# A convolution stage on one core: variances queued a step ahead of their powers, and logits written to another PSUM bank

## The chip, the core and the metric

The kernel runs on one core of a Trainium2 chip. The core has five engines that work in parallel and meet through semaphores: TensorE (PE in the profile; PEld is its loading of weights), VectorE (DVE), ScalarE (ACT), GpSimd (POOL) and SyncE (SP), which issues most of the DMAs. Each engine takes its instructions in the order in which they were queued: one that waits holds up all behind it. The metric is the device time of one execution in microseconds; lower is better.

## What is computed

Four layers, each a normalized input that goes through a block and is added to the residual:

```python
x = x + _L0_xattn_ref(_layernorm(x), L0_xattn_k, fside_S2_0, ctx_2048, ctx_2048, 8)
x = x + _L0_ffn_ref(_layernorm(x), L0_ffn_gate_w, ...)     # 8 experts, the best 2 of each token, and a shared one
x = x + _L1_xattn_ref(_layernorm(x), ctx_2048, itok_BxS_0_1023, ...)
x = x + _L1_ffn_ref(_layernorm(x), L1_ffn_proj1, ...)
```

The change lies in the first layer and the router of the second. The first is a long convolution, written in the reference with Fourier transforms:

```python
kv = vr[:, :, :, None, :] * x2r[:, :, None, :, :]
y = irfft(rfft(kv, n=fft_size) * k_f[None, :, None, None, :], n=fft_size)[..., :L]
y = y + kv * skip
out = jnp.einsum('bhijl,bhil->bhjl', y, x1r)
```

The layer norm is `(x - m) / sqrt(v + eps)`. The router's logits are `logits = xf @ gate_w`, 512 by 8.

## The kernel before

Data are 4096 rows of 512. The convolution works on 32 heads, a tile of 128 rows each, and is done as matmuls with a Toeplitz matrix of the filter. A head has two halves (u = 0, 1), and a half four blocks (lb = 0 to 3) of 128 positions. For a block, conv takes 3 matmuls for each of the first two input blocks (high and low parts, line 387) and one full-precision matmul, recorded as two, for each further one (line 382). VectorE then multiplies the result from PSUM (z, line 394) and sums it (line 400).

The inputs of the matmuls are made ahead. GpSimd makes the products kf (line 355), five blocks ahead of their use. ScalarE rounds two of four into kh (line 362), and the remainder kl (line 370) is subtracted by VectorE for the first block and by GpSimd for the second.

In the same queues run, for head h+1, the filter (lines 300 to 312), the norm and the transposes (turn, line 332, into bank PV), for head h+2 the loads and the variance (stats), and for head h-1 the end of the layer: finish transposes the result into bank PR (line 405) and adds it to the residual (line 407). Its output is normalized again for the router: stats0 makes the variance, shift0 the shift nm0 (line 472), norm0 the rows xb (line 476), turn0 transposes them into PV (line 483). A head later logit multiplies them by the gate (line 490, into PV) and ScalarE copies the 8 logits out (line 492); best takes the largest (lines 501, 502), and choose, in heads 9, 17 and 25, turns eight tiles of them into experts and gates.

A variance is three VectorE instructions (lines 120 to 122: statistics over 512 elements, their aggregate, plus epsilon) and a GpSimd power of -0.5 (line 123). layernorm_stats queues all four at once, in stats at u = 1, lb = 2, and in stats0 at u = 1, lb = 0.

The order is that of the Python loop over h, u and lb: each step calls the functions, and each call appends to its engine's queue. Dependencies are tokens (a semaphore and its value). `T` and `U` keep the last token under a name; `U["PV",]` and `U["PR",]` hold the last reader of the two banks, for which the next writer waits. After the last head a second loop (line 791 on) starts the shared expert, with the remains of the convolution queued as events between its steps; there PR also takes the transposes of line 631 (turn1), and line 638 empties it.

Of the kernel before, what the change touches and what calls it, by code (L numbers as in the profile page):

```python
# [11 lines left out]
ALU = mybir.AluOpType  # L12
ACT = mybir.ActivationFunctionType
# [5 lines left out]
EPS = 1e-5  # L19
# [92 lines left out]
def make_identity(p, ident):  # L112
    a = p.do("gpsimd", lambda e: e.memset(ident, 0.0))
    return p.do("gpsimd", lambda e: e.affine_select(out=ident, in_=ident, compare_op=ALU.not_equal, fill=1.0, base=0,
                                                    pattern=[[-1, 128]], channel_multiplier=1), a)


def layernorm_stats(p, x, st, ag, rs, mhalf, tok, free, c):

    a = p.do("vector", lambda e: e.bn_stats(st, x), tok, free)  # L120
    a = p.do("vector", lambda e: e.bn_aggr(ag, st), a)
    a = p.do("vector", lambda e: e.tensor_scalar(rs, ag[:, 1:2], EPS, None, ALU.add), a)
    return p.do("gpsimd", lambda e: e.tensor_tensor(rs, rs, mhalf, ALU.pow), a, c)
# [3 lines left out]
def front_phase(nc, ctx, d, before, xa, idx, gat, ident, mhalf, n_heads=NHC):  # L127


    p = Phase(nc, ctx, "c", before)  # L130
    keep = Mem(nc, ctx, "f")
    LAG, NG, NB, RING = 5, NT // 2, 4, 5
    U = {}

    def gu(*k):
        return U.get(k)
# [27 lines left out]
    xt = m.sb("xt", [128, 4, 512])  # L164
# [85 lines left out]
    T = {}  # L250
# [5 lines left out]
    def clear(n):  # L256

        for c in left[:n]:
            U["clr",] = p.dma("sync", dz, lambda e, c=c: e.dma_start(xsz[:, c:c + 512], zero[:, :]), c_z)
        del left[:n]  # L260

    def g(*k):
        return T.get(k)
# [27 lines left out]

    def stats(h):
        s = h % 2
        T["rs", h] = layernorm_stats(p, xt[:, h % 4, :], st[:, s, :], ag[:, s, :], rs[:, s, :], mhalf, g("x", h), g("xn", h - 2), c_mh)

    def filt(h):

        s = h % 2
        if h < 2:
            T["pt", h] = p.do("tensor", lambda e: e.matmul(PT[:, :], anti, tf[:, s, :], start=True, stop=True), g("tf", h), c_an, g("tl", h - 1))  # L300
        else:
            T["pt", h] = p.do("tensor", lambda e: e.matmul(PT[:, :], antir, tr[:, s, 0, :], start=True, stop=True), g("tf", h), c_anr, g("tl", h - 1))
        T["th", h] = p.do("scalar", lambda e: e.activation(th[:, s, :], PT[:, :], ACT.Copy), g("pt", h), g("mm", h - 2))
# [10 lines left out]
    def shift(h):  # L314
        s = h % 2
        T["nm", h] = p.do("vector", lambda e: e.tensor_scalar(nm[:, s, :], ag[:, s, 0:1], rs[:, s, :], -1.0, ALU.mult, ALU.mult), g("rs", h), g("xn", h - 2))
# [85 lines left out]
    def finish(h):  # L402
        s = h % 2
        for lb in range(4):
            T["pr", h] = p.do("tensor", lambda e, lb=lb: e.transpose(PR[:, 128 * lb:128 * lb + 128], R[:, s, lb, :], ident),
                              g("R", h), gu("PR"), inc=lb == 3)
        T["out2", h] = U["PR",] = p.do("vector", lambda e: e.tensor_tensor(xt[:, h % 4, :], sk[:, s, :], PR[:, :], ALU.add), g("pr", h), g("sk", h))
        T["out", h] = p.dma("sync", do[h % 4], lambda e: e.dma_start(d["x1"][:, 8 * h:8 * h + 8, :], xt[:, h % 4, :]), g("out2", h))
# [56 lines left out]

    def stats0(i):
        s = i % 2
        U["rs", i] = layernorm_stats(p, xt[:, i % 4, :], st0[:, s, :], ag0[:, s, :], rs0[:, s, :], mhalf, T["out2", i], gu("xb", i - 2), c_mh)

    def shift0(i):  # L470
        s = i % 2
# [15 lines left out]
    def logit(i):  # L487

        for k in range(4):
            U["pl", i] = p.do("tensor", lambda e, k=k: e.matmul(PV[:, 0:8], xT[:, k, :], gw[:, k, :], start=k == 0, stop=k == 3),  # L490
                              U["xT", i], U["c0",], gu("PV"), inc=k == 3)
        U["lg", i] = U["PV",] = p.do("scalar", lambda e: e.activation(lg[:, i // 8 % 2, i % 8, :], PV[:, 0:8], ACT.Copy), U["pl", i], gu("ix", i - 16))

    B8 = [128, 8, 8]

# [180 lines left out]
    load(0)  # L676
    load(1)
    stats(0)
    filt(0)
    filt_lo(0)  # L680
    shift(0)
# [3 lines left out]
    skips(0)  # L685
    residual(0)
    stats(1)
    shift(1)
    split_filters()
    setup()  # L690
# [5 lines left out]
    for h in range(n_heads):  # L696
        more = h + 1 < n_heads
        for u in range(2):
            for lb in range(4):
                if u == 0 and lb == 2 and h + 2 < n_heads:  # L700
                    load(h + 2)
                    clear(3)
                if u == 1 and lb == 2 and h + 2 < n_heads:
                    stats(h + 2)
                if u == 1 and lb == 0 and more:
                    filt(h + 1)
                if u == 1 and lb == 2 and more:
                    filt_lo(h + 1)
                if u == 0 and lb == 0 and more:
                    norm(h + 1)  # L710
                if u == 0 and lb == 0 and more:
                    weigh(h + 1)
                if u == 1 and lb == 3 and h + 2 < n_heads:
                    shift(h + 2)
                if u == 0 and lb == 3 and more:
                    turn(h + 1)
                n = (2 * h + u) * 4 + lb + 4
                if n + 1 < len(units):
                    product(*units[n + 1])
                if n < len(units):  # L720
                    parts(*units[n], low=False)
                conv(h, u, lb, units[n] if n < len(units) and lb == 0 else None)
                if u == 0 and lb == 3 and h:
                    finish(h - 1)
                if u == 1 and lb == 1 and more:
                    skips(h + 1)
                if u == 1 and lb == 2 and more:
                    residual(h + 1)
                if u == 0 and lb == 1:
                    shared_weights()  # L730
                    if h > 1:
                        logit(h - 2)
                if u == 0 and lb == 3 and h > 1:
                    best(h - 2)
                if u == 1 and lb == 0 and h > 8 and h % 8 == 1:
                    choose(h // 8 - 1)
                if h and u == 1:
                    (stats0, shift0, norm0, turn0)[lb](h - 1)
                if not more and u == 0:
                    fill(row(lb))  # L740
                if not more and u == 1:
                    if lb < 2:
                        loadr(lb)
                    if lb in (1, 2):
                        turn1(lb - 1)
# [14 lines left out]
    def more(n):  # L760
# [6 lines left out]
        if todo:  # L767
            src, to, c = todo.pop(0)
            pend.append((fetch(src), to, c, ("w1",) if to is w1f else ("w2",)))

    events = {0: [lambda: finish(last), lambda: logit(last - 1), lambda: stats0(last), lambda: shift0(last), lambda: norm0(last)], 1: [lambda: best(last - 1)],
              3: [lambda: turn0(last)], 4: [lambda: logit(last)], 5: [lambda: best(last), lambda: choose(3)], 7: [ranks], 8: [offsets],
              9: [places, by_head], 10: [experts], 11: [biases]}
    steps = NG * NB
# [973 lines left out]
```

How the kernel before makes its waits and increments, by code:

```python
    def emit(self, e, eng):  # L72
        seen = {}
        def wait(sem, v):
            if seen.get(id(sem), 0) < v:
                eng.wait_ge(sem, v)
                seen[id(sem)] = v
        for sem, v in self.before:
            wait(sem, v)
        for fn, waits, inc in self.q[e]:
            for w in waits:
                if w is not None:
                    wait(*w)
            ins = fn(eng) if fn else None
            if inc:
                ins.then_inc(*inc)
# [1638 lines left out]
                def run(eng, e=e):  # L1727
                    for p in phases:
                        p.emit(e, eng)
                    if e == "sync":
                        for sem, v in before:
                            eng.wait_ge(sem, v)
```

## Time and profile before

| | |
|---|---|
| median of 3 runs | 3270.91 us (3270.78 to 3271.13) |
| profiled execution, its own time | 3268.49 us |
| its span in the profile | 3266.7 us |
| mean granted TensorE clock over the span | 0.991 |
| PE busy | 3162.6 us (97%) |
| VectorE busy | 2159.1 us (66%) |
| ScalarE busy | 1261.4 us (39%) |
| GpSimd busy | 1126.1 us (34%) |

The convolution stage takes about the first 640 us, a fifth of the span. In its stretch from 300 to 400 us PE is busy 97.09 us, VectorE 87.11, GpSimd 77.22 and ScalarE 33.53, at a granted clock of 1.00. Percentages of the whole span say little of it: GpSimd's 34% is 77% here. A busy PE is not PE at its peak, because matmuls are pipelined and their ends are modelled; the distance between the starts of two matmuls is what one costs. A head is one period of this stage, so one period, read on all four engines, stands for some twenty. The queries read are the waits of an engine (whom it waited for, in all and how often), the timeline of an engine (instructions in order of time, with the idle time ahead and who ended it), and the account of a single line.

### The profile page before, as it was taken

How to read it: one execution, taken by the hardware profiler on the slowest of the kernel's cores; microseconds unless marked ns; L12 is line 12 of the kernel's file. 1: busy time of each engine (PE TensorE's matmuls, PEld its weight loads, DVE VectorE, ACT ScalarE, POOL GpSimd, SP SyncE). 2: the span in 40 equal slices, each digit the busy share in tenths (PEclk: the TensorE clock that was granted, in tenths of full speed). 3: DMA queues.
4: the chain of work that ended last, by engine and by line, in shares of the span. 5: the costliest groups of instructions: out<-in, count | busy, mean ns of one | idle time of the engine just before them, and what ended most of it. 6: DMA issues, size and time to landing. Idle time of an engine off the chain costs nothing.

```text
span 3266.7 us, 51561 instructions
## 1 busy us (share of the span) xinstructions
PE 3162.6 (97%) x18517; PEld 2687.2 (82%) x18517; DVE 2159.1 (66%) x5741; ACT 1261.4 (39%) x3041; POOL 1126.1 (34%) x1179
## 2 busy tenths in 40 slices
PE   7999999999999789999999999999998999999999
PEld 4666666689899579999999999999997888888887
DVE  6888888755555568877788888877776533333332
ACT  2333333333444345555555555555554311111111
POOL 6877777535344322222222222222201011000110
PEclk9999999999999899999999999999999999999999
DMA  4544443269677721111111111111101300000000
GB/s 127 151 142 140 132 133 103 81 198 328 214 234 225 242 72 53 46 46 46 46 46 46 45 38 42 46 46 46 34 14 55 98 26 26 26 26 26 26 14 14
DMA packets 129418, 285.92 MB, mean 88 GB/s; under 512 B 18840, under 2 KB 19488, under 8 KB 129168
## 3 DMA queue, kind: packets, MB, share of 16 engines
q1 hardware_dynamic: 100080, 186.49, 18.3%
q0 software_dynamic: 29088, 96.13, 8.9%
q8 instruction: 153, 2.51, 0.3%
q14 instruction: 97, 0.79, 0.1%
HBM read 177.98 MB, written 104.58 MB: 86 GB/s over the span
## 4 chain that ended last, share of the span: by engine, by line
PE 79%; DVE 9%; POOL 7%; DMA 2%; ACT 1%; issue 1%; SPq 0%; POOLq 0%; DVEq 0%
PE g_PH L1021 11%; PE g_O L1044 11%; PE t_U L1486 10%; PE t_S L1438 9%; PE t_PO L1473 5%; PE t_M L1422 5%; PE t_T L1460 3%; POOL c_kf L355 3%; PE f_Y L664 2%; PE f_Y L893 2%; PE t_M L1377 2%; PE f_Y L387 2%; PE f_Y L382 2%; DVE c_R L400 2%; DVE c_z L394 2%; PE t_M L1359 2%
## 5 line engine op out<-in xcount | busy, mean ns | idle before, releaser
L1448 ACT ACTIVATE t_pr<-t_sm,t_nb 128x256 f32<-128x256 f32 x512 | 256.6, 502 | 368.2 <-DVE t_nb L1444 368.2
L1392 POOL TENSOR_TENSOR t_r<-t_r 128x256 f32<-128x256 f32 x128 | 96.1, 751 | 778.9 <-DVE t_rw L1454 451.4
L1034 DVE CAST g_hh<-g_hf 128x512 fp32r<-128x512 f32 x128 | 61.8, 482 | 435.7 <-PE g_O L1044 427.0
L355 POOL TENSOR_TENSOR c_kf<-c_vt,c_ct 128x512 f32<-128x512 f32 x256 | 297.0, 1181 | 0.0
L1033 ACT ACTIVATE g_hf<-g_PH,g_b1s 128x512 f32<-128x512 f32 x128 | 88.2, 689 | 519.1 <-PE g_PH L1021 518.3
L1455 DVE TENSOR_SCALAR t_pr<-t_pr,t_rw 128x256 f32<-128x256 f32 x512 | 222.0, 434 | 18.1
L387 PE MATMUL f_Y<-c_kh,c_th 128*128 128x512 f32 x448 | 200.1, 447 | 10.5 <-ACT c_kh L362 10.5
L1021 PE MATMUL g_PH<-g_xh,g_w1h 128*128 128x512 f32 x512 | 205.8, 402 | 1.5 <-DVE g_xl L1009 1.5
L1021 PE MATMUL g_PH<-g_xh,g_w1l 128*128 128x512 f32 x512 | 203.5, 397 | 0.0
L1021 PE MATMUL g_PH<-g_xl,g_w1h 128*128 128x512 f32 x512 | 203.1, 397 | 0.0
L1044 PE MATMUL g_O<-g_w2h,g_hh 128*128 128x512 f32 x512 | 202.4, 395 | 0.0
L1044 PE MATMUL g_O<-g_w2h,g_hl 128*128 128x512 f32 x512 | 202.2, 395 | 0.0
L1486 PE MATMUL t_U<-t_voh,t_otl 128*128 128x512 f32 x512 | 201.7, 394 | 0.0
L1486 PE MATMUL t_U<-t_voh,t_oth 128*128 128x512 f32 x512 | 201.7, 394 | 0.0
L1044 PE MATMUL g_O<-g_w2l,g_hh 128*128 128x512 f32 x512 | 201.5, 394 | 0.0
L1486 PE MATMUL t_U<-t_vol,t_oth 128*128 128x512 f32 x512 | 200.9, 392 | 0.0
L1444 DVE CUSTOM_DVE_ANT_0 t_sm<-t_S,t_mk 128x256 f32<-128x256 f32 x512 | 194.6, 417 | 8.6 <-PE t_S L1438 8.6
L394 DVE TENSOR_TENSOR c_z<-f_Y,c_ct 128x512 f32<-128x512 f32 x256 | 174.0, 680 | 35.2 <-PE f_Y L382 35.0
L382 PE MATMUL f_Y<-c_kf,c_t 128*128 128x512 f32 x384 | 185.4, 591 | 0.0
L1465 DVE TENSOR_TENSOR t_ptl<-t_T,t_pth 128x512 fp32r<-128x512 f32 x256 | 175.5, 685 | 15.0 <-ACT t_pth L1464 14.8
L400 DVE TENSOR_REDUCE c_R<-c_z 128x64 f32<-128x512 f32 x256 | 174.9, 683 | 6.6
L387 PE MATMUL f_Y<-c_kl,c_th 128*128 128x512 f32 x448 | 178.1, 398 | 0.0
(345 smaller groups left out, 9706.6 us busy)
## 6 DMA issues: line engine op xcount, KB each, us to landing
xs<-c_zero SPq DMA_DIRECT2D x71, 256.0 KB, 5.2
f_xg<-xs SPq DMA_DIRECT2D x71, 256.0 KB, 3.4
ys<-f_yt POOLq DMA_DIRECT2D x71, 256.0 KB, 3.6
c_tr<-kpad SPq DMA_DIRECT2D x60, 256.0 KB, 4.7
f_xg<-xn SPq DMA_DIRECT2D x40, 256.0 KB, 4.7
c_xt<-x SPq DMA_DIRECT2D x32, 256.0 KB, 3.5
c_cr<-ctx SPq DMA_DIRECT2D x32, 256.0 KB, 4.0
c_ct<-ctxh SPq DMA_DIRECT2D x32, 256.0 KB, 4.1
```

What stands on the lines that cost most here:

```text
L355: T["kv", h] = T["kv1", n] = p.do("gpsimd", lambda e: e.tensor_tensor(o, iv, ic, ALU.mult), g("vt", h), g("ct", h), g("kl", n - 8), g("kh" ...
L382: last = p.do("tensor", lambda e, c=c, mb=mb: e.matmul(Y[y % 4][:, :], t0[:, s, c], kf[:, v, mb, :], start=False, stop=mb == lb), g("t0", ...
L387: last = p.do("tensor", lambda e, a=a, b_=b_, c=c, mb=mb, i=i: e.matmul(Y[y % 4][:, :], a[:, s, c], b_[:, v, mb, :], start=(mb == 0 and i ...
L394: T["z", h] = T["z1", y] = p.do("vector", lambda e: e.tensor_tensor(zz.rearrange("p (b j i) -> p b j i", i=8, j=8), iv, ic, ALU.mult), las ...
L400: T["red", y] = T["R", h] = p.do("vector", lambda e: e.tensor_reduce(rr, zr, AXX, ALU.add), g("z1", y), g("pr", h - 2))
L1021: T["ph", n] = p.do("tensor", lambda e, kk=kk, a=a, b_=b_, i=i: e.matmul(ph[:, :], a[:, k, kk, :], b_[:, s, kk, :], start=i == 0, stop=i = ...
L1044: tk = p.do("tensor", lambda e, a=a, b_=b_, t=t, fin=fin, c=c, beg=beg: e.matmul(O[t][:, :], a[:, n % 2, c], b_[:, k, :], start=beg, stop= ...
L1438: a = p.do("tensor", lambda e, t=t, j=j, q=q, k=k: e.matmul(PS1[:, 256 * t:256 * t + 256], q, k[:, s, :], start=j == 0, stop=j == 4), g("q ...
L1444: T["am", N] = am = p.do("vector", lambda e, t=t, k4=k4: e.tensor_tensor_reduce(out=sm[:, k4, :], in0=PS1[:, 256 * t:256 * t + 256], in1=m ...
L1448: T["ex", x] = p.do("scalar", lambda e, t=t, k4=k4: e.activation(pr[:, N % 2, t, :], sm[:, k4, :], ACT.Exp, bias=nb[:, k4, 0:1], scale=-1. ...
L1455: T["nm", x] = p.do("vector", lambda e, t=t, k4=k4: e.tensor_scalar(pr[:, N % 2, t, :], pr[:, N % 2, t, :], rw[:, k4, 1:2], None, ALU.mult ...
L1486: a = p.do("tensor", lambda e, t=t, tt=tt, j=j, o=o, w=w: e.matmul(PU[t][:, :], o[:, N % 3, tt], w[:, h, :], start=h == 0 and j == 0, stop ...
```

## The change

layernorm_variance is new: the three VectorE instructions of a variance without its power. stats and stats0 now queue only these, and new functions power and power0 queue the power on GpSimd. In the loop stats(h+2) moves from u = 1, lb = 2 to u = 1, lb = 1, and power(h+2) takes its old place. stats0(h-1) moves from u = 1, lb = 0 to directly behind finish(h-1) at u = 0, lb = 3, ahead of best, and power0(h-1) takes its old place. Shifts, norms and transposes stay where they were. The matmuls of logit and the copy behind them go to PR in place of PV. Before the loop and in the events the power follows its variance directly, as before. layernorm_stats stays for the later layers.

```diff
+def layernorm_variance(p, x, st, ag, rs, tok, free):
+
+    a = p.do("vector", lambda e: e.bn_stats(st, x), tok, free)
+    a = p.do("vector", lambda e: e.bn_aggr(ag, st), a)
+    return p.do("vector", lambda e: e.tensor_scalar(rs, ag[:, 1:2], EPS, None, ALU.add), a)
...
     def stats(h):
         s = h % 2
-        T["rs", h] = layernorm_stats(p, xt[:, h % 4, :], st[:, s, :], ag[:, s, :], rs[:, s, :], mhalf, g("x", h), g("xn", h - 2), c_mh)
+        T["va", h] = layernorm_variance(p, xt[:, h % 4, :], st[:, s, :], ag[:, s, :], rs[:, s, :], g("x", h), g("xn", h - 2))
+
+    def power(h):
+        s = h % 2
+        T["rs", h] = p.do("gpsimd", lambda e: e.tensor_tensor(rs[:, s, :], rs[:, s, :], mhalf, ALU.pow), T["va", h], c_mh)
...
     def stats0(i):
         s = i % 2
-        U["rs", i] = layernorm_stats(p, xt[:, i % 4, :], st0[:, s, :], ag0[:, s, :], rs0[:, s, :], mhalf, T["out2", i], gu("xb", i - 2), c_mh)
+        U["va", i] = layernorm_variance(p, xt[:, i % 4, :], st0[:, s, :], ag0[:, s, :], rs0[:, s, :], T["out2", i], gu("xb", i - 2))
+
+    def power0(i):
+        s = i % 2
+        U["rs", i] = p.do("gpsimd", lambda e: e.tensor_tensor(rs0[:, s, :], rs0[:, s, :], mhalf, ALU.pow), U["va", i], c_mh)
...
         for k in range(4):
-            U["pl", i] = p.do("tensor", lambda e, k=k: e.matmul(PV[:, 0:8], xT[:, k, :], gw[:, k, :], start=k == 0, stop=k == 3),
-                              U["xT", i], U["c0",], gu("PV"), inc=k == 3)
-        U["lg", i] = U["PV",] = p.do("scalar", lambda e: e.activation(lg[:, i // 8 % 2, i % 8, :], PV[:, 0:8], ACT.Copy), U["pl", i], gu("ix", i - 16))
+            U["pl", i] = p.do("tensor", lambda e, k=k: e.matmul(PR[:, 0:8], xT[:, k, :], gw[:, k, :], start=k == 0, stop=k == 3),
+                              U["xT", i], U["c0",], gu("PR"), inc=k == 3)
+        U["lg", i] = U["PR",] = p.do("scalar", lambda e: e.activation(lg[:, i // 8 % 2, i % 8, :], PR[:, 0:8], ACT.Copy), U["pl", i], gu("ix", i - 16))
...
+                if u == 1 and lb == 1 and h + 2 < n_heads:
+                    stats(h + 2)
                 if u == 1 and lb == 2 and h + 2 < n_heads:
-                    stats(h + 2)
+                    power(h + 2)
...
                 if u == 0 and lb == 3 and h:
                     finish(h - 1)
+                    stats0(h - 1)
...
                 if h and u == 1:
-                    (stats0, shift0, norm0, turn0)[lb](h - 1)
+                    (power0, shift0, norm0, turn0)[lb](h - 1)
```

## Rows read from the trace of the kernel before

**Rows 1.** PE's waits, first 1300 us: who waited for whom: total, times, longest.

```profile
PE f_PV L332 <- ACT c_lg L492: 14.2, 29, 1.2
PE f_PV L483 <- ACT c_xb L476: 1.0, 3, 0.3
```

**Rows 2.** Timeline of PE: start, us, instruction, [idle before and who ended it].

```profile
50.38 1.02 PE L382 MATMUL f_Y<-c_kf,c_t 128*128 128x512 f32 x2
51.23 0.60 PE L332 MATMUL f_PV<-ident,c_xn 128*128 128x128 f32 x4
...
397.10 1.02 PE L382 MATMUL f_Y<-c_kf,c_t 128*128 128x512 f32 x2
398.40 0.63 PE L332 MATMUL f_PV<-ident,c_xn 128*128 128x128 f32 x4 [0.28 <-ACT c_lg L492]
```

**Rows 3.** GpSimd's waits, first 1300 us.

```profile
POOL c_rs L123 <- DVE c_rs L122: 145.7, 63, 9.5
```

**Rows 4.** Timelines of PE and ScalarE behind the last head.

```profile
648.42 0.50 PE L645 MATMUL f_PSK<-f_xh,c_sw 128*128 128x256 f32 x2 [2.68 <-ACT f_hf L653]
...
658.62 0.64 PE L631 MATMUL f_PR<-ident,f_xg 128*128 128x128 f32 x4
658.80 0.18 ACT L492 ACTIVATE c_lg<-f_PV 128x8 f32<-128x8 f32 x1 [2.65 <-PE f_PV L490]
```

**Rows 5.** Timeline of VectorE, an ordinary head.

```profile
402.18 0.69 DVE L394 TENSOR_TENSOR c_z<-f_Y,c_ct 128x512 f32<-128x512 f32 x1 [0.87 <-PE f_Y L382]
403.51 0.68 DVE L407 TENSOR_TENSOR c_xt<-c_sk,f_PR 128x512 f32<-128x512 f32 x1
...
405.04 0.68 DVE L370 TENSOR_TENSOR c_kl<-c_kf,c_kh 128x512 fp32r<-128x512 f32 x1
406.24 0.68 DVE L120 BATCH_NORM_STATS2 c_st<-c_xt 128x6 f32<-128x512 f32 x1
407.17 0.15 DVE L122 TENSOR_SCALAR c_rs<-c_ag 128x1 f32<-128x1 f32 x1
407.25 0.68 DVE L394 TENSOR_TENSOR c_z<-f_Y,c_ct 128x512 f32<-128x512 f32 x1
409.16 0.21 DVE L472 TENSOR_SCALAR c_nm<-c_ag,c_rs 128x1 f32<-128x1 f32 x1
```

**Rows 6.** Timelines of PE and VectorE, the transposes of line 483 and what precedes them.

```profile
362.87 0.69 DVE L394 TENSOR_TENSOR c_z<-f_Y,c_ct 128x512 f32<-128x512 f32 x1 [0.87 <-PE f_Y L382]
371.27 0.20 DVE L472 TENSOR_SCALAR c_nm<-c_ag,c_rs 128x1 f32<-128x1 f32 x1
372.38 0.66 PE L483 MATMUL f_PV<-ident,c_xb 128*128 128x128 f32 x4 [0.32 <-ACT c_xb L476]
...
392.26 0.60 PE L483 MATMUL f_PV<-ident,c_xb 128*128 128x128 f32 x4
411.21 0.60 PE L483 MATMUL f_PV<-ident,c_xb 128*128 128x128 f32 x4
```

**Rows 7.** Timeline of VectorE behind the last head: a variance directly on its sum.

```profile
643.04 0.69 DVE L407 TENSOR_TENSOR c_xt<-c_sk,f_PR 128x512 f32<-128x512 f32 x1 [0.88 <-PE f_PR L405]
643.76 0.69 DVE L120 BATCH_NORM_STATS2 c_st<-c_xt 128x6 f32<-128x512 f32 x1
```

**Rows 8.** Timeline of GpSimd, the same ordinary head.

```profile
407.41 0.55 POOL L123 TENSOR_TENSOR c_rs<-c_rs,mhalf 128x1 f32<-128x1 f32 x1 [4.06 <-DVE c_rs L122]
407.92 1.07 POOL L355 TENSOR_TENSOR c_kf<-c_vt,c_ct 128x512 f32<-128x512 f32 x1
```

**Rows 9.** VectorE and GpSimd together; last, line 370's durations: ns min/median/max, first and last start.

```profile
14.03 0.75 DVE L325 SCALAR_TENSOR_TENSOR c_w<-c_xn,c_skip,c_cr 128x512 f32<-128x512 f32 x1 [0.88 <-ACT c_xn L320]
...
393.73 1.29 POOL L346 TENSOR_TENSOR c_sk<-c_sk,c_xt 128x512 f32<-128x512 f32 x1
394.23 1.34 DVE L325 SCALAR_TENSOR_TENSOR c_w<-c_xn,c_skip,c_cr 128x512 f32<-128x512 f32 x1
...
L370 DVE TENSOR_TENSOR c_kl<-c_kf,c_kh x64: 679/876/955, 26.4 to 624.8; 128x512 fp32r<-128x512 f32 x64
```

More of the change, by code:

```diff
@@ L678, in front_phase @@
     stats(0)
+    power(0)
     filt(0)
@@ L687, in front_phase @@
     stats(1)
+    power(1)
     shift(1)
@@ L769, in more @@
             pend.append((fetch(src), to, c, ("w1",) if to is w1f else ("w2",)))
-    events = {0: [lambda: finish(last), lambda: logit(last - 1), lambda: stats0(last), lambda: shift0(last), lambda: norm0(last)], 1: [lambda: best(last - 1)],
+    events = {0: [lambda: finish(last), lambda: logit(last - 1), lambda: stats0(last), lambda: power0(last), lambda: shift0(last), lambda: norm0(last)], 1: [lambda: best(last - 1)],
               3: [lambda: turn0(last)], 4: [lambda: logit(last)], 5: [lambda: best(last), lambda: choose(3)], 7: [ranks], 8: [offsets],
```

## The prediction

> **What bounds the kernel now.** I read the waits of TensorE (PE) first, because PE is busy nearly all of the time: what it waits for is what there is to gain. In the convolution stage (27 to 640 us) one wait recurs: the first transpose of a head's values (line 332) waits 29 times, 14.2 us in all, for ScalarE's copy of the logits (line 492), which must leave bank PV first [rows 1]. The wait is more than it lists, since the ends of matmuls are modelled. Without a stall the transposes start 0.85 us after the pair of matmuls ahead of them (50.38 to 51.23); in head 20 it is 1.30 us (397.10 to 398.40) and the row lists 0.28 of idle [rows 2]. So a stall costs PE the listed idle plus 0.17: 14.2 + 29 x 0.17 = 19.1 us. The second PE wait, the transposes of line 483 for ScalarE's xb, comes 3 times, 1.0 us in all [rows 1], by the same rule 1.0 + 3 x 0.17 = 1.5 us. All stalls that this change can touch cost 20.6 us, or 0.63% of the run.
>
> Why are the logits late? ScalarE takes its work in order, and ahead of that copy stand two copies of kf (kh, line 362) that wait for GpSimd. GpSimd waits 145.7 us in 63 waits for the variance (line 122), which is nearly all its idle time [rows 3]: its power (line 123) stands behind a VectorE sum that was queued only a moment earlier. So GpSimd is late, kh is late, the logits are late, and PE waits.
>
> **The new bank.** Logits go to PR. PR's last user is then the residual sum (line 407) of half a head earlier, long done, and the transposes of line 332 need no logits any more; the next user of PR, the transposes of line 405, comes just ahead of z, over 3 us later than line 332 (398.40 to 402.18) [rows 2, 5], when the copy has ended. This alone removes the 19.1 us. It costs something only in the tail: logits of the last head are followed at once by transposes into PR (line 631). They start at 658.62, while the copy runs from 658.80 for 0.18 [rows 4]; they must now wait until about 659.05. I take 0.45 us, between 0.2 (if part is hidden) and 0.9 (the copy's own wait doubled). The logits of head 30 now wait for the residual sum of head 31 as well, about 1.0 us; PE idles 2.68 us soon after for a reason that stays [rows 4], which hides it. Without that cover it would be 1.0 us.
>
> **The variances.** No instruction is added; what counts is order. Times below are from the start of VectorE's product z of the fourth block (402.18), which begins as PE ends that block, so it is PE's clock [rows 5]. Call it z. From z the following are fixed on PE: the transposes of line 483 are due at 411.21, z+9.03 [rows 6]. They need xb, xb needs the shift nm0 (line 472), and nm0 stands at z+6.98 (409.16) [rows 5]. Where nm0 is late, the chain is to be seen: nm0 at 371.27, transposes at 372.38, so nm0 + 1.11 [rows 6]. Nm0 may be at z+7.92 at the latest: a cover of 0.94 us.
>
> Ahead of nm0 VectorE had one variance, that of x1 (stats0). Now it has two, since stats(h+2) moves from behind nm0 to ahead of it. A variance takes 406.24 to 407.25 = 1.01 us. And stats0 now follows directly on the sum that it reads, where a step is 0.72 (643.04 to 643.76) [rows 7] in place of 0.60 (half of 405.04 to 406.24, two steps) [rows 5]. Together 1.13, so nm0 is at z+8.11, the transposes at z+9.22, and PE stalls 0.19 us in a head.
>
> **What GpSimd does with its freedom.** The sum of line 407 starts at z+1.33. Stats0 starts at z+2.05, and its last step is 0.93 later (406.24 to 407.17) at z+2.98 [rows 5]. The power follows 0.24 later (407.17 to 407.41), the next product kf 0.51 after that (407.92) and it lasts 1.07 [rows 8]: GpSimd multiplies from z+3.73 to z+4.80. Before, it was idle then. VectorE comes from z+2.98 in 0.08 to the next instruction, and then over the best logits and the next block's product to its kl (line 370): 1.53 between 403.51 and 405.04, less the sum's own step of 0.60, is 0.93. So kl starts at z+3.99 [rows 5]. kl reads two tensors of SBUF. How such an operation fares beside GpSimd is in the trace: line 325 takes 0.75 us beside an idle GpSimd (14.03), but 1.34 when it starts at 394.23, inside a GpSimd sum that runs from 393.73 to 395.02; it ends 0.55 after that sum's end [rows 9]. So it waited for the whole GpSimd operation. kl itself is 0.68 us at least and 0.88 in the median [rows 9], and the one of our place is a short one (405.04, 0.68) because GpSimd was idle [rows 5]. Now it will start 0.26 after a GpSimd product and end at 4.80 + 0.55 = z+5.35 in place of z+4.67: 0.68 us more. All that follows moves with it, nm0 to z+8.79, the transposes to z+9.90: PE stalls 0.87 us in a head. Bounds: 0.19, if kl gets through unharmed, and 1.1, if it waits for all of 1.07 of the product and its own full 0.68 counts from there.
>
> The Trainium skill ("SBUF — State Buffer", section "Who interferes with whom") says the same and speaks against this change: a VectorE instruction with two SBUF inputs contends with a GpSimd instruction that reads SBUF, and whoever issues first keeps the shared interface for its whole length. By this rule, the trace agrees (0.59 us more on line 325), the term is 0.87 a head; a notion of shared bandwidth, which the page rejects, would give a stall between 0.19 and 0.87.
>
> **The sum.** Line 483 comes in heads 1 to 31 (and once in the tail). Heads 30 and 31 have no stats(h+2), so nm0 is 1.01 earlier and there is no stall. In head 1 there are no best logits yet, kl and kf meet almost at once: 0.4 us (0 to 0.87). Heads 9, 17 and 25 also choose experts between kl and nm0: nm0 at 371.27 less z at 362.87 is 8.40, 1.42 more than 6.98 [rows 5, 6], so there the stall is 2.29, and up to 1.1 more if a small two-input operation of the choice meets GpSimd too; I take 2.85. The other 25 heads stall 0.87 each. 25 x 0.87 = 21.8, 3 x 2.85 = 8.5, 0.4, and the tail 0.5: 31.2 us of new stalls against 20.6 removed. Net +10.6 us. Everything else in the 25 heads has room: GpSimd's next product of line 355 must be there when PE ends a fourth block, and it arrives over 1 us early; kh and kl are ready microseconds ahead of PE. After 670 us nothing is changed and the rest moves as a block. The profiled execution took 3268.49 us (span 3266.7), 2.4 below the median of the runs; 3268.5 + 10.6 = 3279.1 for it, and for the median 3270.9 + 10.6 = **3281.5 us**.
>
> **Rivals.**
> 1. *No collision.* GpSimd's product or VectorE's kl yields, or kl gets its turn first. For it: the lead is only 0.26 us, of which VectorE's claim, made as its preceding operation ends, gives back perhaps 0.1. Against it: both paths start at the same instruction (rs, z+2.98), so the lead doesn't drift. Stalls: 25 x 0.19 + 3 x (0.19 + 1.42) + 0.5 = 10.1; net -10.5, 3260.4 us. Faster, 0.32%.
> 2. *Partial collision.* kl loses about 0.3 us: stall about 0.5 in 25 heads, 1.9 in three, 18.8 with the tail; net -2, 3269 us.
> 3. *No stall at line 483 at all*: xb is through in time though two variances stand ahead of it. Only the 20.6 us go: 3251 us. Against it speak the three heads in which nm0 at z+8.40 stalls PE now [rows 6].
> 4. *A worse collision*: the choice's operations and the second variance meet GpSimd as well, 1.1 a head: 25 x 1.1 + 3 x 3.6 + 0.9 = 39; net +19, 3289 us.
> The forecast is itself the slower side: VectorE's path from z to nm0 takes PE's place as the bound. It decides as soon as a head's stall exceeds (20.6 - 0.5 - 3 x 1.42) / 28 = 0.57 us, that is, nm0 later than z+8.49.
>
> **Numbers.** Forecast 0.61 (3276 to 3287); no collision 0.20 (3258 to 3264); partial 0.09; never a stall 0.04; worse 0.06. A measurement of this kernel tells about 0.2% (6.5 us) from no change. Faster 0.25, same 0.12, slower 0.63. The range leaves out the last two rivals and the fast end of the first: 3259 to 3287; the forecast's own range is 3276 to 3287.
>
> **What would show it.** Right: no wait of line 332 for line 492 any more; PE waits of line 483 for xb in some 28 heads, 0.7 listed (0.87 less 0.17); the distance of two heads 19.37 us (before: 18.95, from 392.26 to 411.21 [rows 6]; less the stall of 0.45 that is 18.50, and with the new one 19.37); GpSimd's waits for the variance down from 145.7 to about 100; kl of line 370 at z+4.0 lasting some 1.35 in place of 0.68; line 631 waiting for line 492 once. Wrong: kl at 0.68 and heads 18.7 apart mean rival 1; heads 18.5 apart mean rival 3. If line 332 still waits for ScalarE, the new bank doesn't do what it says. If the heads agree and the total doesn't, the difference arose after 670 us, which I hold to be a block.

## The result, and the profile after

| | before | after |
|---|---|---|
| median of 5 runs beside each other | 3271.13 us (3270.78 to 3277.41) | 3290.61 us (3283.76 to 3291.07) |
| profiled execution, its own time | 3268.49 us | 3290.61 us |
| its span | 3266.7 us | 3288.9 us |
| mean granted clock over the span | 0.991 | 0.988 |

The change makes the kernel slower: the ratio is 1.0052, with an interval of 1.004 to 1.0063 (13 to 21 us). The medians differ by 19.5 us where 10.6 were forecast. The forecast had the side and, in the ordinary heads, the mechanism; the size was too small by 8.9 us, and a step was missing.

Line numbers grow by 11 in the convolution (332 is now 343, 370 is 381, 394 is 405) and by 15 in the code of the values (472 is 487, 476 is 491, 483 is 498, 492 is 507, 501 is 516). The powers have lines 305 (of stats) and 483 (of stats0).

The waits of TensorE (PE) from 0 to 670 us; the columns are who waited for whom, the sum in us, how often, and the longest in us:

```profile
PE f_PV L498 <- ACT c_xb L491: 27.0, 28, 3.2
...
PE f_PR L505 <- DVE c_xt L418: 0.9, 1, 0.9
```

The wait of line 332 for the logits [rows 1] is gone. In its place stands the one that was forecast: the transposes of line 498 wait for xb, 28 times in place of 3. The 0.9 are the logits of head 30, which wait for the residual sum (1.0 was forecast, under cover). The waits of GpSimd in the same stretch:

```profile
POOL c_rs L483 <- DVE c_mx L516: 67.0, 30, 6.0
...
POOL c_rs L305 <- DVE c_rs L122: 19.6, 30, 2.2
POOL c_rs L483 <- DVE c_rs L122: 11.2, 1, 11.2
```

Together these are 97.8 us, where [rows 3] had 145.7. (Releasers are inferred; line 516 stands directly behind the variance on VectorE and is named in its place.) GpSimd did get its work earlier. This is what it met there: one stretch of head 20, with the start, the duration, and in brackets the idle time ahead and who ended it; on GpSimd, VectorE and PE.

```profile
396.65 0.55 POOL L483 TENSOR_TENSOR c_rs<-c_rs,mhalf 128x1 f32<-128x1 f32 x1 [2.10 <-DVE c_mx L516]
397.16 1.06 POOL L366 TENSOR_TENSOR c_kf<-c_vt,c_ct 128x512 f32<-128x512 f32 x1
...
397.42 1.35 DVE L381 TENSOR_TENSOR c_kl<-c_kf,c_kh 128x512 fp32r<-128x512 f32 x1
398.19 1.72 POOL L381 TENSOR_TENSOR c_kl<-c_kf,c_kh 128x512 fp32r<-128x512 f32 x1
...
402.21 0.21 DVE L487 TENSOR_SCALAR c_nm<-c_ag,c_rs 128x1 f32<-128x1 f32 x1
...
403.32 0.66 PE L498 MATMUL f_PV<-ident,c_xb 128*128 128x128 f32 x4 [0.70 <-ACT c_xb L491]
...
409.07 0.60 PE L343 MATMUL f_PV<-ident,c_xn 128*128 128x128 f32 x4
```

VectorE's kl starts 0.26 us after GpSimd's product and takes 1.35 us in place of 0.68 [rows 5]; it ends 0.55 us after that product. The shift nm0 (line 487) starts 1.11 us before the transposes, as in [rows 6], and PE lists 0.70 us of idle time. Line 343 waits for nobody here. Ordinary heads are now 19.38 to 19.40 us apart; 19.37 was forecast. Up to here every step held.

Heads 9, 17 and 25, which also choose experts, did not. They are 23.39, 26.16 and 23.44 us long (a head is counted from one group of transposes of line 416 to the next). Two things are in the trace of head 9. First, the last small operation of the choice:

```profile
215.28 1.27 POOL L381 TENSOR_TENSOR c_kl<-c_kf,c_kh 128x512 fp32r<-128x512 f32 x1 [2.29 <-ACT c_kh L373]
...
215.39 1.19 DVE L534 TENSOR_TENSOR f_gac<-c_sm,f_gac 128x8 f32<-128x8 f32 x1
...
220.53 0.66 PE L498 MATMUL f_PV<-ident,c_xb 128*128 128x128 f32 x4 [3.15 <-ACT c_xb L491]
```

This is a two-input operation on 8 values a partition; the same line takes 0.17 us in the last choice (683.27). It takes 1.19 us here and ends as GpSimd's subtraction kl (line 381) ends, so the stall is 3.15 + 0.17 = 3.32 us, where 2.85 was taken. Second, what PE's matmuls cost after that wait, from PE's timeline:

```profile
221.25 0.40 PE L398 MATMUL f_Y<-c_kh,c_tl 128*128 128x512 f32 x1
221.49 0.40 PE L398 MATMUL f_Y<-c_kl,c_th 128*128 128x512 f32 x1
221.72 0.58 PE L398 MATMUL f_Y<-c_kh,c_th 128*128 128x512 f32 x1
222.10 0.63 PE L398 MATMUL f_Y<-c_kh,c_tl 128*128 128x512 f32 x1
```

and the account of two stretches of 2 us (length, then busy time and instructions of PE, PEld, VectorE, ScalarE and GpSimd, granted clock, DMA share, GB/s):

```profile
222.00:224.00 2.00, 2.00 (x6) 1.53 (x6) 1.83 (x3) 1.67 (x3) 2.00 (x3) 0.50 0.89 240
224.00:226.00 2.00, 2.00 (x12) 1.86 (x11) 2.00 (x4) 0.18 (x1) 2.00 (x2) 0.70 0.98 208
```

The same matmul starts 0.235 us after the one ahead of it at first and 0.43 later: the granted clock is 0.50 (1.2 GHz) from about 221.8, where it was 1.00 (2.4 GHz) all through this stage before. What it costs is what a choosing head is longer than an ordinary one, less the longer wait: 23.39 - 19.39 - (3.15 - 0.70) = 1.55 us in head 9, 4.32 in head 17 and, with a wait of 3.19, 1.56 in head 25, some 7.4 us in all. This is one execution; the five of this kernel took 3283.76 to 3291.07 us, so the cost need not be the same in each.

### The profile page after: what moved, and what is told of

Its sections match the earlier page's. It is cut to its first block, busy times and chain, and to the rows that moved or that the text cites. A ratio compares the mean times of both kernels' runs of the same rounds, so it can differ in the third digit from the quotient of the medians.

```text
span 3288.9 us, 51591 instructions
## 1 busy us (share of the span) xinstructions
PE 3169.1 (96%) x18517; PEld 2690.8 (82%) x18517; DVE 2182.6 (66%) x5741; ACT 1258.6 (38%) x3041; POOL 1138.1 (35%) x1179
## 3 DMA queue, kind: packets, MB, share of 16 engines
q1 hardware_dynamic: 100080, 186.49, 18.1%
## 4 chain that ended last, share of the span: by engine, by line
PE 83%; DVE 10%; DMA 2%; POOL 2%; ACT 1%; issue 1%; SPq 0%; POOLq 0%; DVEq 0%
PE g_PH L1041 11%; PE g_O L1064 11%; PE t_U L1506 10%; PE t_S L1458 9%; PE f_Y L398 6%; PE t_PO L1493 5%; PE t_M L1442 5%; PE t_T L1480 3%; PE f_Y L393 3%; PE f_Y L913 2%; PE f_Y L679 2%; PE t_M L1397 2%; DVE c_R L411 2%; PE t_M L1379 2%; DVE c_z L405 2%; PE f_PSK L882 1%
## 5 line engine op out<-in xcount | busy, mean ns | idle before, releaser
L366 POOL TENSOR_TENSOR c_kf<-c_vt,c_ct 128x512 f32<-128x512 f32 x256 | 286.2, 1132 | 44.9 <-PE f_Y L393 33.4
L1475 DVE TENSOR_SCALAR t_pr<-t_pr,t_rw 128x256 f32<-128x256 f32 x512 | 222.8, 435 | 18.1
L1485 DVE TENSOR_TENSOR t_ptl<-t_T,t_pth 128x512 fp32r<-128x512 f32 x256 | 175.5, 686 | 15.0 <-ACT t_pth L1484 14.8
L398 PE MATMUL f_Y<-c_kh,c_tl 128*128 128x512 f32 x448 | 179.5, 401 | 0.0
```

The source lines that it names most:

```text
L366: T["kv", h] = T["kv1", n] = p.do("gpsimd", lambda e: e.tensor_tensor(o, iv, ic, ALU.mult), g("vt", h), g("ct", h), g("kl", n - 8), g("kh" ...
L398: last = p.do("tensor", lambda e, a=a, b_=b_, c=c, mb=mb, i=i: e.matmul(Y[y % 4][:, :], a[:, s, c], b_[:, v, mb, :], start=(mb == 0 and i ...
L1475: T["nm", x] = p.do("vector", lambda e, t=t, k4=k4: e.tensor_scalar(pr[:, N % 2, t, :], pr[:, N % 2, t, :], rw[:, k4, 1:2], None, ALU.mult ...
L1485: T["ptl", N] = p.do("vector", lambda e: e.tensor_tensor(ptl[:, N % 2, :, :], v, f32(pth[:, N % 2, :, :]), ALU.subtract), T["pth", N], g(" ...
```

## The experiments

All were timed in 5 rounds beside the kernel before. Each diff is against the kernel that is named; "after" is the changed kernel. The theory is: a VectorE operation with two inputs in SBUF waits until a GpSimd product that started ahead of it has ended (A), and it is this, with the second variance, that makes nm0 late.

### The bank alone

Before, with the logits in PR and the variances where they were.

```diff
-            U["pl", i] = p.do("tensor", lambda e, k=k: e.matmul(PV[:, 0:8], xT[:, k, :], gw[:, k, :], ...
+            U["pl", i] = p.do("tensor", lambda e, k=k: e.matmul(PR[:, 0:8], xT[:, k, :], gw[:, k, :], ...
-        U["lg", i] = U["PV",] = ... PV[:, 0:8] ...
+        U["lg", i] = U["PR",] = ... PR[:, 0:8] ...
```

> The kernel before with the logits in PR and nothing else. Theory A (the new bank takes away the stalls of 19.1 us; the loss of the whole change is VectorE's path to nm0, held up by a collision with GpSimd): line 332 waits for nobody, heads are 18.50 apart (before 18.95), line 483 waits only in the three choosing heads, 0.3 listed, kl of line 370 stays at 0.68 beside an idle GpSimd; 3271 - 19 + 0.5 = about 3252 us, ratio 0.994. Theory B (the loss comes from the bank: finish waits for the logits, or PR is in somebody's way): slower than before, and line 405 waits for line 492.

3248.79 us (3245.45 to 3250.34), ratio 0.9936 [0.9923, 0.995]. Ordinary heads are 18.47 us apart, the choosing ones 19.02. PE's waits of that kernel, with before's line numbers:

```profile
PE f_PV L483 <- ACT c_xb L476: 1.0, 3, 0.3
PE f_PR L490 <- DVE c_xt L407: 0.9, 1, 0.9
PE f_PR L631 <- ACT c_lg L492: 0.4, 1, 0.4
```

So the bank's half of the change is worth what the profile of before said for it: 19.1 us of stalls at line 332, less 0.45 in the tail. The last logits come 19.7 us earlier in the profiles (638.12 in place of 657.81), and the medians differ by 20.9 us (before took 3269.66 beside it; the interval is 16 to 25). The 1.0 us of line 483 stays, and the tail pays 0.4 once. This version beats both kernels. Its granted clock is 1.00 throughout the stage, though the choice stands where it stood.

### The variances alone

After, with the logits back in PV.

```diff
-        U["lg", i] = U["PR",] = ... PR[:, 0:8] ...
+        U["lg", i] = U["PV",] = ... PV[:, 0:8] ...
```

> The changed kernel with the logits back in PV: the variances alone. Theory A: GpSimd is early, so kh and the logits are early too and the transposes of values don't wait in spite of the shared bank; heads 19.39 apart and three long stalls of 3.3 us as in the whole change; 3289 to 3291 us, ratio 1.005 to 1.006. Theory B (the bank did the harm): about 3260 us, heads 18.7 apart.

3286.75 us (3284.02 to 3289.31), ratio 1.005 [1.0036, 1.0063]. Heads are 19.40 us apart, the choosing ones 24.45, 26.11 and 23.44. Line 343 does not wait for the logits here either. So the whole loss belongs to the variances, and beside them the bank is worth nothing that these times show. The logits are copied soon enough in the shared bank too. First the kernel before, then this one (matmuls of the logits, their copy, the next transposes into PV; the transposes of before, at 398.40, are in [rows 2]):

```profile
394.81 0.95 PE L490 MATMUL f_PV<-c_gw,c_xT 128*128 128x8 f32 x8
398.10 0.16 ACT L492 ACTIVATE c_lg<-f_PV 128x8 f32<-128x8 f32 x1
...
427.33 0.95 PE L505 MATMUL f_PV<-c_gw,c_xT 128*128 128x8 f32 x8
428.32 0.18 ACT L507 ACTIVATE c_lg<-f_PV 128x8 f32<-128x8 f32 x1 [0.23 <-PE f_PV L505]
...
430.48 0.60 PE L343 MATMUL f_PV<-ident,c_xn 128*128 128x128 f32 x4
```

The copy came 3.29 us behind its matmuls and comes 0.99 behind them now, because ScalarE no longer waits long for GpSimd's products; it has ended 2.0 us before the transposes. The variances alone remove the wait that the bank removes. That is why the effects of the two halves (-21 and +17 us) do not add up.

### Kl ahead of z

After, with VectorE's kl queued ahead of the product z in the second half's first block, so that it no longer meets GpSimd's product.

```diff
-                    parts(*units[n], low=False)
-                conv(h, u, lb, units[n] if n < len(units) and lb == 0 else None)
+                    parts(*units[n], low=u == 1 and lb == 0)
+                conv(h, u, lb, units[n] if n < len(units) and lb == 0 and u == 0 else None)
```

> The changed kernel, but in the second half's first block kl stands ahead of z in VectorE's queue: same instructions, kl starts 0.3 us ahead of GpSimd's product in place of 0.26 behind it. Theory A (whoever starts first keeps the port): kl lasts 0.68, GpSimd's product is the longer one (about 1.3 in place of 1.07), nm0 at z+8.24, stall 0.32, heads 18.8 apart; choosing heads stall 2.7; 3267 us without clock losses, 3275 with those of the whole change, ratio 0.999 to 1.001. Rival C (the two engines slow each other by sharing bandwidth, whatever the order): kl still 1.0 or more, heads above 19.1, 3280 us or more.

3267.72 us (3264.32 to 3268.8), ratio 0.9994 [0.9985, 1.0003]; heads 18.85 us apart, as expected.

```profile
403.62 0.55 POOL L483 TENSOR_TENSOR c_rs<-c_rs,mhalf 128x1 f32<-128x1 f32 x1 [2.10 <-DVE c_mx L516]
...
403.81 0.67 DVE L381 TENSOR_TENSOR c_kl<-c_kf,c_kh 128x512 fp32r<-128x512 f32 x1
...
404.14 1.27 POOL L366 TENSOR_TENSOR c_kf<-c_vt,c_ct 128x512 f32<-128x512 f32 x1
...
404.40 0.68 DVE L405 TENSOR_TENSOR c_z<-f_Y,c_ct 128x512 f32<-128x512 f32 x1
```

Kl comes first now and takes 0.67; it is GpSimd's product that takes 1.27 in place of 1.06. The product z, which reads one input from PSUM, runs beside GpSimd in 0.68. Stalls that remain are 0.1 listed in ordinary heads and 2.6 in the choosing ones, which are 22.73, 21.30 and 21.34 us long.

### The product behind kl

After, with the power of stats0 behind GpSimd's next pair of products, so that VectorE's queue stays as the change has it and only GpSimd's order differs.

```diff
                     parts(*units[n], low=False)
+                if h and u == 1 and lb == 1:
+                    power0(h - 1)
...
-                    (power0, shift0, norm0, turn0)[lb](h - 1)
+                    (lambda i: None, shift0, norm0, turn0)[lb](h - 1)
```

> The changed kernel with the power of stats0 queued on GpSimd behind the next product and remainder in place of ahead of them: GpSimd works through while VectorE makes the variance, and has nothing but the power to do when kl comes. VectorE's queue is exactly that of the changed kernel. Theory A (0.68 of the stall of 0.87 is the collision, 0.19 the second variance): kl 0.68, heads 18.7 apart; choosing heads stall 2.6 and lose clock; 3266 to 3270 us, ratio 0.999 to 1.000. Rival G (the stall is VectorE's longer queue, the long kl only a by-product): heads stay at 19.4.

3266.62 us (3264.25 to 3270.96), ratio 0.9983 [0.9974, 0.9992]; heads 18.71 apart. VectorE and GpSimd at the same place:

```profile
403.71 1.27 POOL L381 TENSOR_TENSOR c_kl<-c_kf,c_kh 128x512 fp32r<-128x512 f32 x1 [0.24 <-ACT c_kh L373]
404.94 0.55 POOL L483 TENSOR_TENSOR c_rs<-c_rs,mhalf 128x1 f32<-128x1 f32 x1
...
405.32 0.68 DVE L381 TENSOR_TENSOR c_kl<-c_kf,c_kh 128x512 fp32r<-128x512 f32 x1
```

VectorE has the same instructions in the same order, and kl has 0.68 again; each head loses 0.68 us of its length (19.39 to 18.71). This is the collision's price alone. The clock falls behind all three choosing heads here (waits of 2.48, 2.48 and 2.53), which are 22.70 to 22.74 us long.

### Each variance back in its place

First after with stats(h+2) back at u = 1, lb = 2:

```diff
-                if u == 1 and lb == 1 and h + 2 < n_heads:
-                    stats(h + 2)
                 if u == 1 and lb == 2 and h + 2 < n_heads:
+                    stats(h + 2)
                     power(h + 2)
```

> The changed kernel with the variance of the loads, stats(h+2), back behind nm0: only stats0 is early. Theory A: the collision of kl stays (kl 1.35), but nm0 is 1.01 earlier, at z+7.78, under the z+7.92 that is free; so no wait of line 498 in ordinary heads, heads 18.5 apart. Choosing heads stall 2.3, with the clock falling behind them at a cost of 1.5 to 4.5 each. 3257 to 3262 us, ratio 0.996 to 0.9975. Rival F (an early stats0 alone is what costs): heads above 19.

3269.23 us (3266.09 to 3272.25), ratio 0.9992 [0.9983, 1.0001]; heads 18.77 to 18.87 us apart, where 18.5 was expected. Kl collides as in the changed kernel (1.35). PE lists 0.17 us of wait for xb in five early heads and none in the ordinary ones from the tenth on; yet most of these are 18.78 us long, 0.31 more than the 18.47 of the kernel with the bank alone. The stall is there all the same; the modelled end of the matmuls ahead hides it:

```profile
436.71 0.60 PE L416 MATMUL f_PR<-ident,c_R 128*128 128x128 f32 x4
...
437.31 0.68 DVE L405 TENSOR_TENSOR c_z<-f_Y,c_ct 128x512 f32<-128x512 f32 x1
...
445.07 0.21 DVE L487 TENSOR_SCALAR c_nm<-c_ag,c_rs 128x1 f32<-128x1 f32 x1
...
446.18 0.66 PE L498 MATMUL f_PV<-ident,c_xb 128*128 128x128 f32 x4
```

The transposes of line 498 start 1.11 us behind nm0, as where they wait for xb, and laid beside the same head of the kernel with the bank alone PE loses its 0.31 us at this place and nowhere else. From VectorE's z to nm0 it is 7.76 us, as expected (7.78). But z starts 0.60 us behind PE's transposes of line 416 here, and 0.20 behind them in the changed kernel (393.23 and 393.43): VectorE is late before the count begins. It is so because GpSimd waits for the second variance, now right behind nm0 on VectorE, and VectorE then waits for kh, which ScalarE makes from GpSimd's late product:

```profile
408.81 0.55 POOL L305 TENSOR_TENSOR c_rs<-c_rs,mhalf 128x1 f32<-128x1 f32 x1 [2.57 <-DVE c_rs L122]
...
414.50 0.88 DVE L381 TENSOR_TENSOR c_kl<-c_kf,c_kh 128x512 fp32r<-128x512 f32 x1 [1.03 <-ACT c_kh L373]
```

VectorE has no other idle time in a head there: it no longer waits for PE ahead of the fourth block's product, as it does in after for 1.54. VectorE, GpSimd and ScalarE seem to form a loop of 18.8 us; this is read from the rows and was not tried on its own. The expectation's 18.5 is wrong because it took VectorE's z for PE's clock; its statement that the second variance costs nm0 1.01 us holds (8.78 from z in the changed kernel, 7.76 here).

Then after with stats0 back at the head of the second half:

```diff
                     finish(h - 1)
-                    stats0(h - 1)
...
                 if h and u == 1:
+                    if lb == 0:
+                        stats0(h - 1)
```

> The changed kernel with stats0 back in its old place, its power behind it: only stats(h+2) is early. Theory A: GpSimd is held by stats0 again until after kl, so kl lasts 0.68 and there is no collision; nm0 at z+7.99, a stall of 0.07 and heads 18.55 apart; choosing heads stall 1.5 without a loss of clock; 3255 to 3259 us, ratio 0.9955 to 0.997. The collision theory fails if kl is still long here, or if kl is 0.68 and heads are 19 apart.

3255.86 us (3251.57 to 3259.19), ratio 0.9953 [0.9939, 0.9967]; heads 18.59, choosing ones 20.02. GpSimd waits for the variance again, its product starts late, and kl is alone:

```profile
396.59 0.55 POOL L483 TENSOR_TENSOR c_rs<-c_rs,mhalf 128x1 f32<-128x1 f32 x1 [3.96 <-DVE c_rs L122]
...
412.82 0.68 DVE L381 TENSOR_TENSOR c_kl<-c_kf,c_kh 128x512 fp32r<-128x512 f32 x1
```

Taking the move of stats0 back is worth 35 us (3290.61 to 3255.86), though this move only makes a variance earlier. That is more than 28 stalls of 0.87: it takes in the three choosing heads and their clock. But neither move does the harm by itself. With the logits in PR, and each beside its own runs of before, the kernel with neither move is 20.9 us faster, with the variance of the loads early 16.5, with stats0 early 3.2, and with both it is 19.5 slower. So early stats0 costs 17.7 us alone and 36.0 beside the other move: the second variance uses up the time that would have covered the collision. The choosing heads stall PE here for 1.33 us as listed, and the clock stays at 1.00 from 100 to 600 us.

### Where the clock went

The account of the choosing heads left 7.4 us that were seen but not explained. After, with the choice three blocks later:

```diff
-                if u == 1 and lb == 0 and h > 8 and h % 8 == 1:
+                if u == 1 and lb == 3 and h > 8 and h % 8 == 1:
                     choose(h // 8 - 1)
```

> The changed kernel with the choice of experts queued in the last block of the second half, behind nm0, in place of the first. Theory D (of the 19.5 us lost, some 15 belong to the three choosing heads: a stall 2.45 us longer than elsewhere, and TensorE's clock at 0.50 for 3 to 9 us after it): the choosing heads are 19.39 apart like the others, the granted clock is 1.00 there, 3275 to 3279 us, ratio 1.0015 to 1.0025. Rival E (the clock falls at those places for another reason than the long stall): the clock still falls between 200 and 560 us, and 3284 us or more.

3281.07 us (3278.55 to 3290.11), ratio 1.0038 [1.0025, 1.0052], a miss. The wait for xb is 0.7 everywhere, but ScalarE's exponential of the choice now stands ahead of the copy xT, and two small VectorE operations are held by GpSimd on the way to it:

```profile
221.06 0.95 DVE L524 CAST c_sm<-c_ix 128x16 f32<-128x16 uint32 x1
222.04 0.99 DVE L525 TENSOR_TENSOR c_sm<-c_mx 128x8 f32<-128x8 f32 x1
...
223.81 1.60 PE L505 MATMUL f_PR<-c_gw,c_xT 128*128 128x8 f32 x8 [1.76 <-ACT c_xT L500]
225.26 0.77 PE L398 MATMUL f_Y<-c_kh,c_th 128*128 128x512 f32 x1
225.84 0.63 PE L398 MATMUL f_Y<-c_kh,c_tl 128*128 128x512 f32 x1
```

A new long wait, and the clock fell after it (0.63 for a matmul in place of 0.40). The profile is of an execution of 3289.47 us, 8.4 above the median, so what the clock costs there need not be typical. This tells nothing against the theory that a long wait lowers the clock, and doesn't show it either. Next, the choice behind norm0 in the third block:

```diff
-                if u == 1 and lb == 0 and h > 8 and h % 8 == 1:
-                    choose(h // 8 - 1)
...
                     (power0, shift0, norm0, turn0)[lb](h - 1)
+                if u == 1 and lb == 2 and h > 8 and h % 8 == 1:
+                    choose(h // 8 - 1)
```

> The changed kernel with the choice of experts in the third block of the second half, behind nm0 and behind ScalarE's xb. Unlike the try in the last block, ScalarE's exponential then hardly holds up the copy that the logits wait for. Theory D: no PE wait above 1 us in the choosing heads, the granted clock stays at 1.00 from 100 to 600 us, heads 9, 17 and 25 are at most 20 us apart from the next; 3274 to 3279 us, ratio 1.001 to 1.003. If the clock still falls without a long wait, the clock losses have another cause.

3285.42 us (3281.35 to 3288.28), ratio 1.0045 [1.0031, 1.0058], a miss for the same reason. Three of the choice's operations, each 0.17 to 0.22 in the changed kernel, waited for GpSimd products one after another:

```profile
218.65 0.99 DVE L525 TENSOR_TENSOR c_sm<-c_mx 128x8 f32<-128x8 f32 x1
219.56 1.15 DVE L528 TENSOR_TENSOR c_oh<-c_iota,c_sm 128x64 f32<-128x64 f32 x1
220.64 1.10 DVE L529 TENSOR_TENSOR c_oh<-c_iota,c_sm 128x64 f32<-128x64 f32 x1
```

VectorE carried the 4 us into the next head, whose transposes waited 2.91, and there the clock fell. Last, the choice cut in three parts (copy, difference and exponential; the comparisons and their sum; the gates), one in each of three following heads, at a place where VectorE waits for PE anyway:

```diff
+    def choose_a(c):
...
+        d_ = G["d"] = p.do("vector", lambda e: e.tensor_copy(S_[:, :, 0:2], I[:, :, 0:2]), U["ix", 8 * c + 7])
...
+    def choose_b(c):
...
+    def choose_c(c):
...
-                if u == 1 and lb == 0 and h > 8 and h % 8 == 1:
-                    choose(h // 8 - 1)
+                if u == 0 and lb == 2 and h > 8 and h % 8 in (2, 3, 4):
+                    (choose_a, choose_b, choose_c)[h % 8 - 2](h // 8 - 1)
```

> The changed kernel with the choice (lines 524 to 534) cut in three parts, one part in each of the heads 10/11/12, 18/19/20 and 26/27/28, each issued behind the third block's reduction in the first half of the head, where VectorE has 2.1 us to wait for TensorE before its next product. Nothing of it stands ahead of the variances any more. Theory C (the clock's 7.6 us belong to the long wait that the choice makes in the changed kernel): every head 19.39 us apart, the wait for xb 0.7 us in all 28 heads, granted clock 1.00 throughout 100 to 600; the excess of the three choosing heads, 4.00 + 6.77 + 4.05 = 14.8 us, goes: 3290.6 - 14.8 = 3275.8. Theory D (the clock falls now and then in this kernel whatever the choice does, for example from the 0.7 us waits together): only the stall's part goes, some 7 us, and the clock still shows 0.50 somewhere between 200 and 600: 3283.4. Rival E (the choice costs its VectorE time wherever it stands): heads 10 to 12 and their like are up to 2 us longer, 3281.

3274.75 us (3272.96 to 3278.99), ratio 1.0011 [1.0002, 1.002]. From the second head to the thirtieth every head is 19.38 to 19.40 us long, the wait for xb is 0.7 in all of them, and the clock is back. PE's waits, and the account of two stretches of 100 us:

```profile
PE f_PV L498 <- ACT c_xb L491: 19.7, 28, 0.7
```

```profile
200.00:300.00 100.00, 96.47 (x410) 67.15 (x408) 90.58 (x173) 33.95 (x60) 78.78 (x74) 1.00 0.47 139
300.00:400.00 100.00, 96.49 (x405) 66.73 (x406) 89.56 (x167) 31.78 (x58) 78.78 (x73) 1.00 0.48 139
```

Nothing but the choice was moved, and 15.9 us went at the medians, of which the lengths of the heads account for 14.8: 7.4 of stall and 7.4 of the clock. The waits of 0.7 us, all 28 of them, do not lower it. The first theory's 3275.8 holds, the others' 3281 and 3283.4 do not.

The same cut in the kernel with the bank alone (the diff is the one above, against that kernel):

> The kernel before with the logits in the bank of the transposed x, and the choice cut in three parts as in the run beside this one. The choosing heads of that kernel without the cut were 0.54 us longer than the others, three times: 3248.8 - 1.6 = 3247.2, ratio 0.993, if the parts lie in VectorE's wait for TensorE; if VectorE is what these heads wait for in their first half, the parts cost up to 1 us each, nine times: 3256.

3258.52 us (3256.12 to 3261.61), ratio 0.9961 [0.9948, 0.9975]: worse than that kernel without the cut. There VectorE has 0.39 us to wait for PE in an ordinary head, where the changed kernel has 1.55 (2.1, as the expectation said, only right behind a choosing head), and the heads with the parts are up to 1.56 longer:

```profile
PE f_PV L483 <- ACT c_xb L476: 5.7, 6, 1.3
```

This is the second case of the expectation, 3256. A place is free only as long as its own slack is there.

## Why the prediction was right or wrong

- **What bounds the kernel, and the bank's gain.** Right. 19.1 us less 0.45 in the tail were read for the bank; the bank alone brought 19.7 in the profiled stage and 20.9 at the medians. The tail lists 0.36 against 0.45 taken. What the prediction did not say is that the other half takes the same wait away.
- **The cover of nm0 (0.94 us) and the second variance (1.13).** Right: nm0 + 1.11 is the transposes' start in after too. With the collision taken away, heads are 18.71 apart, 0.21 above the prediction's unstalled 18.50 and 0.24 above the measured 18.47; the prediction had 0.19 for just that.
- **The collision, 0.68 us a head.** Right, and shown from both sides: with kl before z, and with the product behind kl, kl takes 0.67 and 0.68 again and a head is 0.54 and 0.68 shorter, and the second of the two changes nothing in VectorE's queue. The rule that was weighed there (the Trainium skill, "SBUF — State Buffer", section "Who interferes with whom") is borne out, by 1.35 against 0.68 for kl; a shared bandwidth is not.
- **Ordinary heads.** 19.37 forecast, 19.39 measured. GpSimd's waits about 100 forecast, 97.8 measured.
- **Head 1.** 0.4 taken, no stall found: the second head comes 18.47 after the first.
- **The three choosing heads.** This is the term that failed. It was 3 x 2.85 = 8.5 us. Above 18.50 they are 4.89 + 7.66 + 4.94 = 17.5 us long, so it was short by 9.0, about the whole error of the forecast (8.9). Of this, 0.47 + 0.47 + 0.51 = 1.45 is the size of the stall: the small operation at line 534 met GpSimd in full, which the prediction had named and weighed with half its price. The other 7.4 is a step that was missing. The prediction counted a stall of PE as the stall, with the matmuls behind it at the speed of the rows of before. Behind a wait of over 3 us they ran at half the clock and took 1.6 to 4.3 us more.
- **"After 670 us the rest moves as a block".** In the convolution +10.6 was forecast. The last logits come at 676.04 us in place of 657.81, so +18.2: 10.6 + 1.45 + 7.4 - 0.4 of head 1 - 1.0 from the start of the stage is 18.1. The spans differ by 22.2. The remaining 4 us arose after the convolution, where no instruction was changed. From the last logits to the end, the profiled executions of all kernels here took 2605.6 to 2612.9 us (before 2608.9, after 2612.9), with no relation to what was edited. So this is not put down to the change, and its cause stays open. Its size is partly cancelled at the medians, because the profiled execution of before was 2.6 below its median: 18.1 + 4.0 - 2.6 = 19.5. That the 9.0 of the choosing heads and the 8.9 of the whole agree so well is therefore chance: the -1.4 and the +1.4 beside them cancel.
- **The rivals.** No collision, partial collision and no stall at all are excluded by the heads' 19.39. The fourth, a worse collision, gave 3289 for a reason that didn't hold in the 25 ordinary heads. It held in three, and its time is near the measured one by the clock, not by its own sum.

What lowers the clock stays in part open. The runs show after which waits it fell, and not why. The choice itself is not enough: with the bank alone, and with stats0 back in its place, it stands in the same block of the same heads, and the clock stays at 1.00.

## What to carry to other kernels

Work that is made earlier for a waiting engine moves that engine's other work as well: ask what it will then start, and which operation of a neighbour starts just behind it. Here 1 us more on VectorE and 0.7 us of a collision turned a gain of 21 us into a loss of 17 to 20. Price a stall of PE in a stage that runs at the full clock not only by its length: try whether it can be cut in short pieces, since 28 stalls of 0.7 us cost their length, and three of 3.15 us cost half as much again, once over twice as much.

Of two edits that were made together, run each alone before judging them: the worse half takes away by itself the wait that the better one removes, so the gain of the better one can't be seen in the two together.

## What the runs showed of the hardware

- A VectorE operation with two SBUF inputs waits for a GpSimd operation that began ahead of it even if it is tiny: 128x8 values took 0.88 to 1.21 us in place of 0.17, 128x64 took 1.10 to 1.16 in place of 0.22, and a cast of 128x16, which has one input, took 0.95 in place of 0.16. The trace shows no wait there, only a long duration. The loser depends on who starts first: when kl was first (403.81), the GpSimd product took 1.27 in place of 1.06.
- The granted clock fell to 0.50 behind all three waits of PE of 3.15 to 3.19 us (after), all three of 2.91 to 2.93 (the choice behind norm0) and all three of 1.76 to 1.77 (the choice three blocks later, with a wait of 0.71 some 4.5 us ahead of each); in after this cost 1.6 to 4.3 us each. It did not fall behind 28 waits of 0.7 nor behind three of 1.33. Of nine waits of 2.48 to 2.66 it fell behind seven: all six with the product behind kl and with stats(h+2) back, and one of three with kl ahead of z, where the first choosing head is 22.73 us long and the other two 21.30 and 21.34, which is an ordinary head of 18.85 and the longer wait alone. So the length of the wait does not settle it.
